# Layer 0 of a four-layer kernel: the logits' bias as a 65th row, the experts' bias sums out of the routing, the output part inside the recurrence's stage

## The reference, cut to what matters

```
# attention branch (a gated delta rule, 16 heads of 8)
q, k, v = silu(conv(xn @ W + b)), q and k divided by their norms
alpha, beta, out_gate = sigmoid(xn@Wa+ba), sigmoid(xn@Wb+bb), silu(xn@Wg+bg)
for t:  S = a*S + b * (v - a*S k) k^T ;  o_t = S q_t
mu, var = mean and mean square minus mu^2 of o, per head, over all tokens
y = (o - mu) * rsqrt(var + 1e-5) * gn_scale + gn_bias
attention = (out_gate * y) @ Wo + bo
# expert branch (8 experts, the best two of each token)
h = gelu(layernorm(xn @ Wr1 + br1)) ;  logits = h @ Wr2 + br2        # 64 -> 8
w = softmax(logits) cut to its two largest and renormalised
experts = sum_e w_e * ((x1_e * gelu(x2_e)) @ W2[e] + b2[e]),  x1_e, x2_e = halves of xn @ W1[e] + b1[e]
x = x + attention + experts
```

## Time and profile before

| | us |
|---|---|
| median of three runs | 2067.01 |
| the profiled execution's own time | 2066.19 |
| its span, from the first to the last instruction | 2064.4 |
| routing stage | 41.7 to 84.4 |
| the two projection stages | 85.2 to 161.9 |
| recurrence and experts, until the next stage starts | 162.7 to 539.6 |
| load of `Wo`, and the output | 539.6 to 559.3 |
| layer 1 starts | 560.4 |

### The profile page before, as it was taken

How to read it: one execution, slowest core, us unless ns; L and a number is a source line. 1 busy time by engine, 2 the same in 40 slices (tenths; PEclk the granted TensorE clock), 3 DMA queues, 4 the chain that set the end, 5 groups by cost and what they waited for, 6 DMA issues and landing times. The chain is left out here.

```text
span 2064.4 us, 30821 instructions
## 1 busy us (share of the span) xinstructions
PE 1729.7 (84%) x10655; PEld 1118.2 (54%) x10655; DVE 1427.2 (69%) x2106; ACT 1198.2 (58%) x2024; POOL 1132.3 (55%) x1023
## 2 busy tenths in 40 slices
PE   6647999999578587676888999899999999999988
PEld 3314777789443366443553555555555555555564
DVE  3656777763255588665238888888888888888883
ACT  4373333336246376234347877778787777777860
POOL 1234455523200466211334788888888888888881
PEclk8678999997689899897999999999999999999999
DMA  3102222221000000002213999989989899999983
GB/s 76 29 27 84 73 82 82 78 67 32 24 14 0 13 1 1 0 1 81 76 45 66 164 165 158 157 153 159 159 163 161 156 164 164 161 161 158 165 159 61
DMA packets 632550, 193.08 MB, mean 94 GB/s; under 512 B 591601, under 2 KB 624130, under 8 KB 632398
## 3 DMA queue, kind: packets, MB, share of 16 engines
q1 hardware_dynamic: 624006, 167.56, 44.9%
q0 software_dynamic: 8224, 23.51, 3.7%
q10 hardware_dynamic: 168, 0.06, 0.0%
HBM read 36.90 MB, written 12.48 MB: 24 GB/s over the span
## 5 line engine op out<-in xcount | busy, mean ns | idle before, releaser
L2966 DVE TENSOR_REDUCE half_max<-scores 128x1 f32<-128x1024 f32 x512 | 614.8, 1219 | 134.3 <-PE scores L2748 129.0
L2665 POOL TENSOR_TENSOR p_low<-p,p_high 128x2048 f16<-128x2048 f32 (+15 forms) x256 | 576.1, 2250 | 153.2 <-ACT p_high L2892 130.3
L2748 PE MATMUL scores<-k_high,q_pair 128*128 128x512 f16 x1024 | 303.7, 378 | 68.6 <-ACT p L2877 63.9
L2877 ACT ACTIVATE p<-scores,exp_bias 128x1024 f32<-128x1024 f32 (+7 forms) x384 | 317.4, 861 | 68.5 <-DVE exp_bias L2971 66.0
L2892 ACT ACTIVATE p_high<-p 128x2048 f16<-128x2048 f32 (+15 forms) x256 | 282.6, 1104 | 43.5 <-DMA pT_high<-p_high 33.2
L2748 PE MATMUL scores<-k_low,q_pair 128*128 128x512 f16 x1024 | 304.2, 379 | 0.0
L2768 PEld LDWEIGHTS scores<-v_pair,pT_high 128*128 128x128 f16 x2176 | 149.4, 98 | 104.1 <-issue 59.2
L2768 PE MATMUL scores<-v_pair,pT_low 128*128 128x129 f16 x2176 | 183.8, 220 | 9.9 <-DMA pT_low<-p_low 9.3
L2768 PE MATMUL scores<-v_pair,pT_high 128*128 128x129 f16 x2176 | 186.4, 220 | 3.5 <-DMA pT_high<-p_high 3.2
L2768 PEld LDWEIGHTS scores<-v_pair,pT_low 128*128 128x128 f16 x2176 | 145.1, 98 | 44.9 <-DMA pT_low<-p_low 13.8
L2748 PEld LDWEIGHTS scores<-k_low,q_pair 128*128 128x128 f16 x1024 | 99.2, 97 | 121.7
(11 more groups left out here) (499 smaller groups left out, 3257.2 us busy)
## 6 DMA issues: line engine op xcount, KB each, us to landing
pT_high<-p_high SPq DMA_TRANSPOSE x256, 3.6
pT_low<-p_low SPq DMA_TRANSPOSE x256, 3.7
slots<-zero_row SPq DMA_DIRECT2D x1, 3036.0 KB, 14.1
slot_rows<-slots SPq DMA_DIRECT2D x23, 132.0 KB, 2.4
slots_out<-expert_out SPq DMA_DIRECT2D x23, 128.0 KB, 1.8
w_up<-in_L_ffn_inter_w_dram SPq DMA_DIRECT2D x1, 2048.0 KB, 9.1
x_tokens<-in_L_attn_x_dram SPq DMA_DIRECT2D x4, 256.0 KB, 3.4
dispatched<-moe_rows SPq DMA_DIRECT2D x1, 1024.0 KB, 11.5
```

Source lines behind the costliest of these rows:

```text
L2665: pool.tensor_tensor(flat(pl[:, buf, b0:b0 + n, :]), flat(p32[:, buf, b0:b0 + n, :]), flat(ph[:, buf, b0:b0 + n, :]), ALU.subtract).then_i ...
L2748: mm = pe.matmul(ps[:, b.start + i, :], q, k[:, par, cs(2 * half + i)], start=start, stop=not start)
L2877: act.activation(flat(p32[:, buf, b0 + first:b0 + first + w, :]), flat(ps[:, banks(p, half), :])[:, 0:w * P], ACT.Exp, bias=bias[:, p:p + ...
L2966: dve.tensor_reduce(mx[:, p % 2, half:half + 1], flat(ps[:, b[half], :]), AX.X, ALU.max, negate=True)\
```

## The change

1. The router's hidden tile gets a 65th row of ones, set by POOL in the stage of the hidden layer. `Wr2` and `br2` are loaded into one tile of 65 rows. One matmul per tile gives the logits, and L477 goes.
2. The product with `b2` (L503) and its addition to `m.x` (L582) leave the routing. SP stores `wT` to DRAM there, and loads it again at the end of `l0_recur` into the place of expert weights that are no longer needed.
3. The pick of `b1` (L593, L595) moves to the second stage of `l0_project`, ahead of DVE's wait for beta.
4. `l0_output` goes. Its work stands at the end of the lists of `l0_recur`: SP loads `Wo` after the first three loads of slot rows, POOL gathers both choices of a tile one after the other with one semaphore per quarter, PE starts the output sums with the `b2` product and then takes a quarter at a time, ACT uses Ln and Exp in place of Sqrt and reciprocal, and DVE centres and gates by quarters.

```diff
 (l0_route)
+                sp.wait_ge(w_copied, 1)
+                sp.dma_start(r.wT, wT[:]).then_inc(w_stored, 16)
+                sp.wait_ge(w_stored, 16)
...
-                    pe.matmul(logits[:, n, :], h[0:R, n * P:(n + 1) * P], wr2, start=True, stop=False)
-                    mm = pe.matmul(logits[:, n, :], m.ones[0:1, :], br2, start=False, stop=True)
+                    mm = pe.matmul(logits[:, n, :], h[0:R + 1, n * P:(n + 1) * P], w.r2[:], start=True, stop=True)
...
-                for c in range(NCH):
...
-                    pe.wait_ge(w_copied, 1)
-                    pe.matmul(rps[:, c % 2, :], w.b2[:], wT[:, cs(c)], start=True, stop=True).then_inc(b_sum, 1)
...
-                for c in range(NCH):
-                    dve.wait_ge(b_sum, c + 1)
-                    dve.tensor_tensor(m.x[:, cs(c)], m.x[:, cs(c)], rps[:, c % 2, :], ALU.add).then_inc(routed, 1)
...
 (l0_project, second stage)
                 dve.tensor_copy(bab_col[:], ps[:, 0, 0, 0:2]).then_inc(bias_ready, 1)
+                TX = [P, TILES, 2 * FT, EXPERTS]
+                dve.tensor_tensor(bw, w.b1[:].rearrange("p e s t -> p (s t) e").unsqueeze(1).to_broadcast(TX),
+                                  w.oh[:].unsqueeze(2).to_broadcast(TX), ALU.mult).then_inc(bias_spread, 1)
+                dve.wait_ge(bias_spread, 1)
+                dve.tensor_reduce(r.b1[:], bw, AX.X, ALU.add).then_inc(bias_picked, 1)
                 dve.wait_ge(b_ready, NCH)
...
 (l0_recur, SP)
+                sp.dma_start(wo[:], inp["L0_attn_Wo"]).then_inc(wo_loaded, 16)
...
                 sp.wait_ge(stored1, 16 * (TILES // 2))
+                sp.wait_ge(down, TILES)
+                sp.dma_start(wT, r.wT).then_inc(wT_loaded, 16)
+                sp.wait_ge(wT_loaded, 16)
 (POOL)
-                    k, n = divmod(i, NT)
+                    n, k = divmod(i, 2)
+                    at = k * NT + n
...
 (PE, after the last carry)
+                pe.wait_ge(hid_ready, PARTS)
+                pe.wait_ge(out_ready, 2 * TILES)
+                pe.wait_ge(features, TILES)
+                pe.wait_ge(wT_loaded, 16)
+                for c in range(NCH):
+                    pe.matmul(po[c], r.b2[:], wT[:, cs(c)], start=True, stop=False)
+                pe.wait_ge(summed, 2)
+                pe.matmul(up[:, 0, 0:2], m.head_ones[:], st[:, 0:2], start=True, stop=True).then_inc(over_heads, 1)
+                pe.wait_ge(wo_loaded, 16)
+                for c in range(NCH):
+                    pe.wait_ge(gathered[c], 16 * 2 * (NT // NCH))
+                    for n in range(4):
+                        for k in range(2):
+                            pe.matmul(po[c][:, n * P:(n + 1) * P], r.rows[:, k, 4 * c + n, 0:P], m.ident[:], start=False, stop=False)
+                    pe.wait_ge(gated, c + 1)
+                    pe.matmul(po[c], wo[:], r.o[:, cs(c)], start=False, stop=True).then_inc(projected, 1)
 (ACT)
+                act.preload_act_table_set(LN_EXP)
+                act.wait_ge(o_ready, NCH)
+                act.activation(r.wo[:, 1, :], r.o[:], ACT.Square, accum_out=st[:, 1:2]).then_inc(summed, 1)
+                act.wait_ge(eps_set, 1)
+                act.wait_ge(var_ready, 1)
+                act.activation(st[:, 4:5], st[:, 4:5], ACT.Ln, bias=epst[:]).then_inc(logged, 1)
+                act.wait_ge(logged, 1)
+                act.activation(st[:, 4:5], st[:, 4:5], ACT.Exp, scale=-0.5).then_inc(inverted, 1)
 (DVE: the sum over o, four small instructions for mean and variance, one for the scale, then)
+                for c in range(NCH):
+                    dve.tensor_scalar(r.o[:, cs(c)], r.o[:, cs(c)], st[:, 5:6], st[:, 6:7], ALU.add, ALU.mult).then_inc(centered, 1)
+                    dve.wait_ge(centered, c + 1)
                     dve.scalar_tensor_tensor(out=r.o[:, cs(c)], in0=r.o[:, cs(c)], scalar=m.col("L0_attn_gn_bias"),
                                              in1=r.gate[:, cs(c)], op0=ALU.add, op1=ALU.mult).then_inc(gated, 1)
 (layer0_router)
+            @block.gpsimd
+            def _(pool):
+                pool.memset(h[R:R + 1, :], 1.0).then_inc(one_set, 1)
```

More of the change, by code:

```diff
@@ L391, with l0_weights @@
 ROW = P + 4
-def l0_weights(nc, own, inp):
+def l0_weights(nc, own, inp, b2):
     sb = lambda name, shape: own.enter_context(sbuf(nc, name, shape))
@@ L590, in _ @@
                                               op1=ALU.add))
[L591 to L595, removed]
+                dve.tensor_tensor(oh[:], place[:].unsqueeze(1).to_broadcast(TE), ex[:, 1, :].unsqueeze(2).to_broadcast(TE),
+                                  ALU.is_equal).then_inc(routed, 1)
 def l0_project(nc, m, r, w):
@@ L802, in l0_recur @@
                    "t_zeroed", "scaled", "d_blocks", "p_turned", "p_blocks", "s_blocks", "t_next", "t_ready", "carried", "o_ready",
-                   "risen", "activated", "hid_ready", "down", "out_ready", "stored0", "stored1") as (
+                   "risen", "activated", "hid_ready", "down", "out_ready", "stored0", "stored1",
+                   "wo_loaded", "wT_loaded", "gathered0", "gathered1", "gathered2", "gathered3", "eps_set", "summed", "over_heads", "stats",
+                   "var_ready", "logged", "inverted", "centered", "gated", "projected", "added") as (
                 block, z_set, qa_ready, bd_ready, us_ready, os_ready, zs_ready, zks_ready, az_ready,
@@ L807, in l0_recur @@
                 t_zeroed, scaled, d_blocks, p_turned, p_blocks, s_blocks, t_next, t_ready, carried, o_ready,
-                risen, activated, hid_ready, down, out_ready, stored0, stored1):
+                risen, activated, hid_ready, down, out_ready, stored0, stored1,
+                wo_loaded, wT_loaded, gathered0, gathered1, gathered2, gathered3, eps_set, summed, over_heads, stats,
+                var_ready, logged, inverted, centered, gated, projected, added):
+            gathered = (gathered0, gathered1, gathered2, gathered3)
             w_loaded, slots, stored = (w_loaded0, w_loaded1, w_loaded2, w_loaded3), (slots0, slots1, slots2), (stored0, stored1)
@@ L1163, in _ @@
                     add_carried(c)
-def l0_output(nc, m, inp, r):
-    with ExitStack() as own:
-        sb = lambda name, shape: own.enter_context(sbuf(nc, name, shape))
-        wo = sb("w_o", [P, P])
-        load_all(nc, [(wo[:], inp["L0_attn_Wo"])])
-        st = sb("stats", [P, 8])
-        sq = sb("o_squared", [P, TOK])
-        ps = own.enter_context(psum(nc, "group_sums", [P, CH]))
-        po = own.enter_context(psum(nc, "out_proj", [P, NCH, CH]))
-        with stage(nc, "summed", "over_heads", "std_ready", "chain", "gated", "projected", "added") as (
-                block, summed, over_heads, std_ready, chain, gated, projected, added):
-            @block.scalar
-            def _(act):
-                act.activation(sq[:], r.o[:], ACT.Square, accum_out=st[:, 1:2]).then_inc(summed, 1)
-                act.wait_ge(chain, 5)
-                act.activation(st[:, 4:5], st[:, 4:5], ACT.Sqrt).then_inc(std_ready, 1)
-            @block.tensor
-            def _(pe):
-                pe.wait_ge(summed, 2)
-                pe.matmul(ps[:, 0:2], m.head_ones[:], st[:, 0:2], start=True, stop=True).then_inc(over_heads, 1)
-                pe.wait_ge(r.gathered, 16 * 2 * NT)
-                for n in range(NT):
-                    c, j = divmod(n, CH // P)
-                    for k in range(2):
-                        pe.matmul(po[:, c, j * P:(j + 1) * P], r.rows[:, k, n, 0:P], m.ident[:], start=j == 0 and k == 0, stop=False)
-                for c in range(NCH):
-                    pe.wait_ge(gated, c + 1)
-                    pe.matmul(po[:, c, :], wo[:], r.o[:, cs(c)], start=False, stop=True).then_inc(projected, 1)
-            @block.vector
-            def _(dve):
-                n = [0]
-                def link(ins):
-                    n[0] += 1
-                    ins.then_inc(chain, 1)
-                    dve.wait_ge(chain, n[0])
@@ L1224, in _ @@
                     dve.wait_ge(projected, c + 1)
[L1225 removed]
+                    dve.scalar_tensor_tensor(out=m.x[:, cs(c)], in0=po[c], scalar=m.col("L0_attn_bo"),
                                              in1=m.x[:, cs(c)], op0=ALU.add, op1=ALU.add).then_inc(added, 1)
@@ L1235, in layer0_router @@
         R = P // 2
-        h = sb("router_hidden", [R, TOK])
-        with psum(nc, "router_up", [R, NCH, CH]) as ps, stage(nc, "up", "biased") as (block, up, biased):
+        h = sb("router_hidden", [R + 1, TOK])
+        with psum(nc, "router_up", [R, NCH, CH]) as ps, stage(nc, "up", "biased", "one_set") as (block, up, biased, one_set):
+            @block.gpsimd
+            def _(pool):
+                pool.memset(h[R:R + 1, :], 1.0).then_inc(one_set, 1)
             @block.tensor
```

80 lines of the change are left out of this document (41 added, 39 removed).

## The result

The changed kernel took 2039.09 us (median of 4 runs, 2033.99 to 2042.16), the kernel before 2068.38 beside it: a ratio of 0.9857 (95% interval 0.9834 to 0.988), 29 us faster. Forecast were 2031, with 2026 to 2038 as range: right direction, 1.1 us outside the range. The profiled execution took 2034.0 us (span 2032.2), 32.2 less than the one of before, where the sum said 36.1.

What follows compares the result with a forecast made beforehand. Bounds taken: layer 0's routing, where DVE waits for logits, and 36.4 us from last carry to layer 1. 8.35 + 10.8 - 0.2 + 17.2 = 36.1 us off 2066.2 gives 2030.1; median 0.8 above: 2031, range 2026 to 2038.

Steps and rivals of the forecast that it cites:

- Logits: Routing of layer 0: 32 of 64 matmul passes go at 0.26 us each, saving 8.35 us (bounds 0 to 8.4).
- Row of ones, pick of `b1`: Hidden-layer and second projection stages: both hidden behind other work, costing nothing; without cover 1.8 and 4.5 us.
- Bias sums out of the routing: Routing ends with SP's store, landing 2.1 us, then 0.85 to the next stage: 10.8 us sooner (6.5 to 11.4).
- POOL's drain: End of the recurrence: drain ends at 538.7 as before, a floor for the stage's end, ahead of the last addition at 542.1.
- Rival 2: Store slow (4.3 us lost) or POOL holds the recurrence stage longer (1.6 more): 2037; chance 0.09.
- rivals 3 and 4: Half clock in recurrence and experts, 2071 or 2091, chance 0.03; zero fill ends routing, front gives nothing, 2050, chance 0.03.
- Output behind the last carry: End of layer 0: full clock 4.5 us after the first `b2` pass, layer 1 at 543.25, 17.2 us sooner.
- tail: End of PE's last carry to layer 1's start: 36.4 us before, about 19 forecast, a gain of 17.2.
- rival 1: Output at half clock because PE waits twice: tail gives 6.6, 2041.6; rise in the middle, some 2035; chance 0.15.
- The rest of the kernel "no change": Later layers: no term in the sum; a shift of the clock's changes may add two or three us of gain.
- the tail's best case: Tail's 18.5 us in the sum 8.4 + 11.4 + 18.5 = 38.3, given for hardly anything lying below 2026.
- front: Routing of layer 0: logits 8.35 and bias sums 10.8 us sooner, before 0.2 for the recurrence's later beginning.

Runs made afterwards that it cites:

- e_store_free: Changed kernel with the first two quarters' rows before `b2`, and the wait for the `wT` store moved to the first projection stage: 2031.61 us, second time 2035.38.
- 13 runs: All runs of the unaltered changed kernel: the first 4 (2039.09 us) and two repeats of 5 (2034.59) and 4 (2033.84); median 2034.6.
- padded kernels: e_store_free with 8 or 16 unused 128-row matmuls behind the last `Wo` product, or three DVE sums instead; run once each: 2035.0, 2036.3 and 2041.9 us.
- e_idle: e_store_free with three sums on DVE behind the last addition; layer 1 starts 6.8 us later after the last carry, layers 1 and 2 take 499.6 us.
- e_front: Kernel before with parts 1 to 3 only; output keeps its two old stages, with the `b2` product there ahead of the rows: 2053.91 us, ratio 0.994.

## Why the prediction was right and wrong

- *Logits: mis-sized, small.* 9.7 us instead of 8.35. I halved 64 passes at 0.26 each; the 32 that stayed take 0.218, at the same granted clock of 0.50. So the 0.26 of passes of 1 row and of 64 rows, in which they alternated, did not hold once only one kind was left, and my upper bound of 8.4 was too low.
- *Row of ones, pick of `b1`: right.* POOL's 1.80 us lie beside `router_up`; the projections take 79.8 instead of 79.7.
- *Bias sums out of the routing: right.* 20.3 - 9.7 = 10.6 instead of 10.8. The store's stretch was 3.37 us from its issue, not 2.95, and is what the stage ends with: SP's wait is over at 64.2, 2.4 us after the issue (2.1 forecast), and 0.9 more pass until PE starts (0.85 forecast). `e_store_free`, which takes the wait away, gains 2.1, and 1.7 the second time. The DMA view of the kernel after, from 61 to 66 us, has the store alone (packets, MB, share of 16 engines):

```profile
DMA packets 16, 0.07 MB, mean 13 GB/s; under 512 B 8, under 2 KB 8, under 8 KB 8
q1 hardware_dynamic: 16, 0.07, 11.1%
```

The packets with data start between 62.5 and 63.0. Their time is 11.1% of 16 engines' 5 us, so 8.9 us, and some 1.1 us for each of eight: the moving itself is about half of the way from the issue to the end of the wait. The Trainium skill's rule on engines per transfer ("DMA: Bandwidth & Descriptors", section "Why a DMA increments its semaphore by 16 and not by 1"), which the prediction cited, gives 8 engines with 8 KB each; 8 of these 16 packets are under 512 B, which leaves 8 with the 64 KB, so the trace agrees. My estimate by its rule, 0.6 us for 8 KB at the zero fill's rate, was too low against these 1.1.
- *POOL's drain: right.* The last gather is issued at 511.18, and POOL's DRAIN ends 7.5 us later at 518.7, as before (7.4) and well ahead of the last addition, which starts at 524.75. In the view of the barrier (ns min/median/max of two, the longest of them the one from 496.6):

```profile
L54 POOLq DRAIN  x2: 34/11048/22062, 496.6 to 526.9; - x2
```

Rival 2 did not happen, nor did rivals 3 and 4: the recurrence took 358.8 us (359.1 before), and the routing gave its 20.3.
- *Output behind the last carry: the step that failed.* "I take 4.5 us from the first wide pass, so 528.5 (bounds 3.9 to 5.5)" was worked out from matmuls with 128 rows (L638, L312, L1193) and applied to `b2`'s with 8. Measured are 13.0 us from the first `b2` pass and 5.4 from the first pass of the rows behind them (5.9 from the small product over the heads). Over all the runs with 128-row passes at the tail's start the distance was 2.8 to 6.1 us, so that the bounds of 3.9 to 5.5 were too narrow even for those. The eight passes took 7.2 us instead of 5.7, the rows of quarter 0 3.76 at half, and each later quarter came as forecast, 2.64 against 2.5. Tail 23.25 instead of 19.25, +4.0. That is rival 1 in its middle form ("if it rises in the middle, some 2035"); but its reason was wrong too. It had put half clock down to PE's waits. That the 13 runs' median of 2034.6 falls on this number is partly luck, as the other misses, -3.0, +1.8, +0.9 and +0.4 (below), cancel.

The row that would have told was in the trace of before, and I didn't put it beside the others: the old `b2` product, eight passes of 8 rows over 512 columns. Its timeline, and the window over it:

```profile
71.59 6.07 PE L503 MATMUL rows_turned<-weights_T,b_down 8*128 8x512 f32 x8 [2.05 <-ACT weights_T L515]
```

```profile
71.60:77.70 6.10, 6.06 (x8) 1.85 (x8) 2.07 (x4) 0.00 (x0) 0.00 (x0) 0.59 0.00 0
```

PE busy for 6.06 of 6.10 us and a mean clock of 0.59: it was at full when the passes began, fell 1.1 us into them (0.50 from 72.8 to 77.7) and was not brought up again. The earlier trace rows gave the same warning, 34.46 of 34.80 us busy at 0.50, and I read it as a rival about waits and not about which passes fill the time.

- *The rest of the kernel "no change": wrong by 3 us.* The prediction let a shift of the clock's changes "in later layers" count for two or three, downwards only. It went upwards, from 495.7 to 498.7. The padded kernels and `e_idle` show that what runs ahead of layer 1 moves it by up to 6 us, without a change in those layers; why it came out as +3 here stays open, and the trace of before gives no sign for it. The same sentence has 18.5 us as the tail's best case, which the prediction works out nowhere; the shortest tail measured, 19.3, is 17.1 less than before.
- *The first set's 2039.* The tail's 4.0 are half of the 8 us between it and the forecast; the median of the kernel's other 9 runs, 2034.0, lies inside the range, and so does the profiled execution. Of the 4 runs only the profiled one, 2034.0, has a trace. How one kernel can take 2030.7 and 2038.9 is shown by `e_store_free`'s two profiled executions, which differ by 5.4 us before the first logits matmul and by 3.0 in layer 3. In the router's layer norm their timelines and windows are, first of the faster, then of the slower one:

```profile
27.57 3.62 PE L312 MATMUL ln_mean<-router_hidden,mean_w 64*64 64x512 f32 x8 [1.44 <-PEq L57]
31.03 3.59 PE L315 MATMUL ln_var<-ln_work,mean_w 64*64 64x512 f32 x8
```

```profile
28.85 5.88 PE L312 MATMUL ln_mean<-router_hidden,mean_w 64*64 64x512 f32 x8 [1.44 <-PEq L57]
34.52 7.03 PE L315 MATMUL ln_var<-ln_work,mean_w 64*64 64x512 f32 x8
```

```profile
26.00:41.00 15.00, 7.18 (x17) 2.05 (x16) 7.61 (x13) 12.76 (x19) 0.00 (x0) 0.92 0.16 22
```

```profile
26.00:41.00 15.00, 13.56 (x19) 3.41 (x17) 5.23 (x9) 8.87 (x13) 0.00 (x0) 0.61 0.16 22
```

The same 16 passes run at full clock in one and, but for the first two or three, at half in the other (0.50 from 31.0 to 41.6). `e_front` and `e_idle` have the late start too (47.0 and 47.3 in the table). The Trainium skill, "TensorE: Matmul & The Clock Gate", section "What's actually happening", says that how many matmuls of one kernel run slow varies from run to run; these two agree, with 5.4 us. Whether the 2038 to 2042 of the first set were such executions stays open, since they left no trace.

The account of the profiled execution against 36.1: front +0.9 (20.3 less 0.2 of a later start, against 19.15), tail -4.0, layers 1 and 2 -3.0, layer 3 +1.8, the rest +0.4: 32.2.

## What to carry to other kernels

When a sum rests on the clock rising, take the rise from a row of passes like the ones that are to bring it up, in rows of weights and data too, and put the passes that have been seen to bring it up first. Trust the changed stages' own rows over the whole time when an edit is worth 2 to 4 us: here the routing and the tail repeated to 0.1 us in three profiles while the kernel's 13 times lay up to 11 us apart. And leave some 3 us on each side for unchanged code behind the change.

## What the runs showed of the hardware that was not expected

- Eight passes of 8 rows over 512 columns, gapless: 7.2 us at half clock and no rise in them. The same with 128 rows: full clock 3.1 us after the first. Once the clock is full, four 8-row passes take 1.98 us (3.78 at half).
- 32 passes of 65 rows over 8 columns: 0.218 us each; alternating 64 rows and 1 row: 0.26; the granted clock was 0.50 in both.
- A 64 KB store from 8 partitions: eight packets of some 1.1 us each, 2.4 us from the issue to the end of the wait for it, and 3.37 to the next stage's first matmul.
- POOL's DRAIN ends 7.4 and 7.5 us after the issue of the last gather, which lands after 2.5; the cause is open.
- Unchanged layers of 495.7 us took 493.6 to 499.6, depending on what ran ahead of them.
